# Four graph layers on one core: the first layer's opening in three pieces of nodes, its degree sums started by copies, its biases loaded behind eight tiles

## The reference

```python
h = relu((x - mean(x)) / sqrt(var(x) + 1e-5)); x = x + relu((adj @ h) @ W0.T + b0)      # layer 0
h = relu(layernorm(x)); x = x + lorentz_attention(h, adj, W1, Wq, Wk, scales)            # layer 1
h = relu(layernorm(x)); x = x + expmap0((adj / deg aggregated logmap(h)) @ W2 + b2)      # layer 2, deg = adj.sum(1)
h = relu(layernorm(x)); x = x + rank_weights(adj != 0) @ (h @ W3) + b3                   # layer 3
```

## Time and profile before

| what | value |
|---|---|
| three runs, us | 1113.17, 1118.21, 1117.3; median 1117.3 |
| profiled execution, us | 1117.34, span 1115.6 |
| granted PE clock, mean | 0.975 |
| busy: PE, DVE, ACT, POOL, us | 1038.4, 865.2, 757.6, 272.7 |
| DMA | 240.42 MB, mean 215 GB/s |
| first layer, tiles 0 to 63 | from 15.15 to 262.8 us |

### The profile page before, as it was taken

One profiled execution on the slowest core, in us unless ns is written; L12 is line 12 of the kernel. 1 busy time (PEld: TensorE's weight loads), 2 busy tenths in 40 slices (PEclk: granted clock), 3 DMA queues, 4 the chain that ended last, 5 costly groups with the idle time before them and its releaser, 6 DMA issues.

```text
span 1115.6 us, 14859 instructions
## 1 busy us (share of the span) xinstructions
PE 1038.4 (93%) x5404; PEld 457.0 (41%) x5404; DVE 865.2 (78%) x1011; ACT 757.6 (68%) x803; POOL 272.7 (24%) x145
## 2 busy tenths in 40 slices
PE   4899999999669999999998998999999998989998
PEld 1233333336643333333333443444544454436544
DVE  6999989996476666688668977877779887778781
ACT  2454554543355666686688889888888888777782
POOL 3179300000010000004005364444343433330010
PEclk9999999998879999999999999999999999989999
DMA  7999999991008888787764444555545545446451
GB/s 264 409 390 351 355 355 317 356 363 56 1 4 298 279 287 283 260 277 272 256 198 140 145 132 158 181 176 170 183 151 189 161 160 189 132 145 223 133 180 39
DMA packets 98438, 240.42 MB, mean 215 GB/s; under 512 B 16449, under 2 KB 47169, under 8 KB 81985
## 3 DMA queue, kind: packets, MB, share of 16 engines
q1 hardware_dynamic: 89152, 222.72, 58.1%
q10 hardware_dynamic: 9216, 16.78, 3.9%
HBM read 221.65 MB, written 17.83 MB: 215 GB/s over the span
## 4 chain that ended last, share of the span: by engine, by line
PE 49%; issue 22%; POOL 13%; DVE 9%; ACT 5%; DMA 1%; SPq 1%; POOLq 0%; DVEq 0%; ACTq 0%
PE PS L555 35%; POOL ring L533 10%; PE PS L701 5%; PE PS L702 5%; POOL H L533 2%; DVE TB L1445 1%; DMA ring<-in_adj_t 1%; ACT work L1105 1%; PE PS L567 1%; DVE work L1894 1%; PE PS L589 1%; PE PS L579 1%; DVE work L1440 1%; PE PS L831 1%; ACT work L1008 1%
## 5 line engine op out<-in xcount | busy, mean ns | idle before, releaser
L1571 DVE TENSOR_TENSOR work<-work,ring 128x1024 f32<-128x1024 f32 x128 | 151.1, 1223 | 78.7 <-ACT work L1105 78.7
L1042 ACT ACTIVATE work<-PS 128x1024 uint8<-128x1024 f32 x128 | 124.1, 1020 | 120.3 <-PE PS L555 120.3
L1105 ACT ACTIVATE work<-PS,att_sc 128x1024 f32<-128x1024 f32 x128 | 147.5, 1201 | 80.3 <-PE PS L702 72.7
L555 PE MATMUL PS<-ring,work 128*65 128x256 f32 (+1 forms) x612 | 194.1, 466 | 2.2 <-DVE work L1922 1.2
L533 POOL TENSOR_TENSOR ring<-work,ring 128x1024 f32<-128x1024 f32 (+1 forms) x57 | 134.0, 2352 | 245.7 <-DVE work L1894 245.6
L555 PE MATMUL PS<-work 128*64 128x512 f32 (+3 forms) x800 | 153.6, 524 | 1.1 <-ACT work L1168 1.0
L1888 DVE SCALAR_TENSOR_TENSOR work<-PS,work 128x1024 f32<-128x1024 f32 x72 | 85.8, 1192 | 56.4 <-PE PS L555 49.9
L555 PEld LDWEIGHTS PS<-ring,work 128*65 128x65 f32 x612 | 83.5, 140 | 91.8 <-issue 66.9
L701 PE MATMUL PS<-work 128*128 128x512 f16 x256 | 98.8, 386 | 4.2 <-DVE work L1394 2.5
L1174 ACT ACTIVATE work<-work 128x1024 f32<-128x1024 f32 x72 | 74.2, 1031 | 37.2 <-DVE work L1882 37.2
L702 PE MATMUL PS<-work 128*128 128x512 f16 x256 | 98.2, 383 | 0.0
(11 more groups left out here) (248 smaller groups left out, 1488.9 us busy)
## 6 DMA issues: line engine op xcount, KB each, us to landing
ring<-in_adj_t SPq DMA_DIRECT2D x96, 1024.0 KB, 5.2
ring<-in_adj_t SPq DMA_DIRECT2D x107, 512.0 KB, 3.8
work<-in_adj_t SPq DMA_DIRECT2D x32, 1024.0 KB, 7.6
codes<-work ACTq DMA_DIRECT2D x64, 256.0 KB, 6.6
ring<-codes SPq DMA_DIRECT2D x64, 256.0 KB, 3.8
H<-in_adj_t SPq DMA_DIRECT2D x25, 512.0 KB, 3.8
X<-in_x SPq DMA_DIRECT2D x2, 512.0 KB, 5.2
out_x<-X SPq DMA_DIRECT2D x1, 512.0 KB, 3.8
```

The source lines that it names most:

```text
L555: return mm(out_ap, lhsT, rhs, start=starts, stop=True, skip_group_check=True)
L1042: nc.scalar.activation(made[:, k, u * UNIT:(u + 1) * UNIT], PS[:, (4 + 2 * u) * BANK:(6 + 2 * u) * BANK], ACT.Relu).then_inc(sem("codes_ma ...
L1105: nc.scalar.activation(att[:, u, :], PS[:, (4 + 2 * u) * BANK:(6 + 2 * u) * BANK], ACT.Sigmoid, bias=att_sc[:, 2:3], scale=att_sc[:, 1:2]) ...
L1571: V.tensor_tensor(prob[:, m % 4, :], att[:, u, :], ring[:, s % RING, u * UNIT:(u + 1) * UNIT], ALU.mult)\
```

## The change

X is loaded and normalised in three pieces, tiles of nodes 24 to 31, 16 to 23 and 0 to 15, and the loads of pieces and adj tiles alternate. PE waits for the pieces at steps 0, 8 and 16. The biases and scalars are loaded behind the eighth tile. The clearing of TB is gone: ACT copies tile 0 into TB and DVE copies tile 32, instead of adding them; all other sums stand two tiles behind their masks, in the loop too. PE runs ten products into an unused PSUM bank before the first tile (`keep_at_work`). The wait of ACT for the scalars moves from behind code 3 to behind code 6. The rest renumbers the semaphore counts of the normalisation.

```diff
+PIECES = ((24, 32), (16, 24), (0, 16))
-            for g in (1, 0):
-                sp.dma_start(grp(X, g), grp(x_nodes, g)).then_inc(sem(f"x_loaded{g}"), 16)
             for k in range(RING0):
+                if k < len(PIECES):
+                    sp.dma_start(piece(X, k), piece(x_nodes, k)).then_inc(sem(f"x_loaded{k}"), 16)
                 sp.dma_start(ring0(k), tile0(0, T - 1 - k)).then_inc(sem(f"adj_loaded{k}"), 16)
-                if k == 1:
-                    for n, bsrc in enumerate((b0, b1, bq, bk, b2, b3)):
-                        sp.dma_start(bias[:, n, :], bsrc.partition_broadcast(P)).then_inc(sem("biases_loaded"), 16)
-                    sp.dma_start(scal[:, :], scalars.partition_broadcast(P)).then_inc(sem("biases_loaded"), 16)
+            for n, bsrc in enumerate((b0, b1, bq, bk, b2, b3)):
+                sp.dma_start(bias[:, n, :], bsrc.partition_broadcast(P)).then_inc(sem("biases_loaded"), 16)
+            sp.dma_start(scal[:, :], scalars.partition_broadcast(P)).then_inc(sem("biases_loaded"), 16)
...
-            nc.gpsimd.memset(TB[:, :], 0.0).then_inc(sem("consts_ready"), 1)
...
+            def keep_at_work(bank):
+                mm(banks(bank, bank + 1), tri_rest[:, :], tri_above[:, :].unsqueeze(1).broadcast_to([P, BANK // P, P]),
+                   start=True, stop=True)
             pe.wait_ge(sem("consts_ready"), 6)
+            for _ in range(10):
+                keep_at_work(7)
...
-                if first and h == 0 or s == TG:
-                    pe.wait_ge(sem("feats0_ready"), 1 + s // TG)
+                if s in (0, TG // 2, TG):
+                    pe.wait_ge(sem("feats0_ready"), 1 + s // (TG // 2))
...
+            square_first(0)
+            root_first(0)
+            square_first(1)
+            one("deg_added", TB[:, 0:HALF], ring0(0), ACT.Copy, ("adj_loaded0", 16))
+            root_first(1)
...
-                    if not h and k == 0:
-                        one("ln_sq", grp(sqr, 0), grp(cen, 0), ACT.Square, ("ln_centred", 2))
-                    if not h and k == 1:
-                        power_of("ln_sd", st[2], st[1], -0.5, "ln_var", 1, (0,))
-                    if not h and k == 3:
+                    if not h and k == 2:
+                        square_first(2)
+                    if not h and k == 5:
+                        root_first(2)
+                    if not h and k == 6:
                         one("scales_ready", esc[:, :], scal[:, 0:3], ACT.Exp, ("biases_loaded", 16 * 7))
...
             mask0(0, 0, 16, True)
             mask0(1, 1, 16, True)
-            centre_first(0)
+            spread_first(1)
             mask0(2, 2, 16, True)
-            degree0(0, 0, 0)
-            spread_first(0)
+            feats_first(1)
             mask0(3, 3, 16, True)
             degree0(0, 1, 1)
-            feats_first(0)
+            sums_first(2)
+            centre_first(2)
             for k in range(4, RING0):
                 mask0(k, k, 16, False)
                 degree0(0, k - 2, k - 2)
-            for k in range(RING0 - 2, RING0):
-                degree0(0, k, k)
+                if k == 5:
+                    spread_first(2)
+            feats_first(2)
...
-                        tile0(h, it * RING0 + (h * T + k), k, it * 16 + (h * T // RING0 + 1) * 16, False)
+                        mask0(it * RING0 + (h * T + k), k, it * 16 + (h * T // RING0 + 1) * 16, False)
+                        degree0(h, it * RING0 + (h * T + k - 2), (k - 2) % RING0)
+            for k in (RING0 - 2, RING0 - 1):
+                degree0(1, 2 * T - RING0 + k, k)
```

More of the change, by code:

```diff
@@ L293, in part, with piece, over_piece @@
             return ap[:, a:b]
+        def piece(ap, n):
+            a, b = PIECES[n]
+            return ap[:, a:b]
+        def over_piece(v, n):
+            a, b = PIECES[n]
+            return piece(v, n).unsqueeze(2).broadcast_to([P, b - a, D])
         def over_part(v, q):
@@ L1023, in norm @@
                 for g in groups:
-                    one("ln_sq", grp(sqr, g), grp(cen, g), ACT.Square, ("ln_centred", L * G + g + 1))
-                power_of("ln_sd", st[2], st[1], -0.5, "ln_var", L * G, groups)
+                    one("ln_sq", grp(sqr, g), grp(cen, g), ACT.Square, ("ln_centred", L * G + 1 + g + 1))
+                power_of("ln_sd", st[2], st[1], -0.5, "ln_var", L * G + 1, groups)
             nc.scalar.preload_act_table_set("natural_log_exp_and_others")
@@ L1032, in flipped_out, with square_first, root_first @@
                 one("flip_out", TA[:, g * UNIT:(g + 1) * UNIT], PS[:, g * UNIT:(g + 1) * UNIT], ACT.Copy, ("flipped", n * G + g + 1))
-            one("ln_sq", grp(sqr, 1), grp(cen, 1), ACT.Square, ("ln_centred", 1))
-            power_of("ln_sd", st[2], st[1], -0.5, "ln_var", 0, (1,))
+            def square_first(n):
+                one("ln_sq", piece(sqr, n), piece(cen, n), ACT.Square, ("ln_centred", n + 1))
+            def root_first(n):
+                act.wait_ge(sem("ln_var"), n + 1)
+                nc.scalar.activation(piece(st[2], n), piece(st[1], n), ACT.Ln).then_inc(sem("act_chain"), 1)
+                chain[0] += 1
+                act.wait_ge(sem("act_chain"), chain[0])
+                nc.scalar.activation(piece(st[2], n), piece(st[2], n), ACT.Exp, scale=-0.5).then_inc(sem("ln_sd"), 1)
+            square_first(0)
[3 more added lines that the diff above has]
+            root_first(1)
             def make_code(h, s, k, at, stored):
@@ L1122, in first_half1 @@
                 if o == 11:
-                    one("ln_sq", grp(sqr, 0), grp(cen, 0), ACT.Square, ("ln_centred", 2 * G + 1))
+                    one("ln_sq", grp(sqr, 0), grp(cen, 0), ACT.Square, ("ln_centred", 2 * G + 1 + 1))
                 if o == 12:
-                    root_of("ln_sd", "ln_var", 2 * G, 0)
+                    root_of("ln_sd", "ln_var", 2 * G + 1, 0)
                 if o == 14:
@@ L1152, in second_half2 @@
                 if n == 8:
-                    one("ln_sq", grp(sqr, 1), grp(cen, 1), ACT.Square, ("ln_centred", 2 * G + 2))
+                    one("ln_sq", grp(sqr, 1), grp(cen, 1), ACT.Square, ("ln_centred", 2 * G + 1 + 2))
                 if n == 9:
-                    power_of("ln_sd", st[2], st[1], -0.5, "ln_var", 2 * G + 1, (1,))
+                    power_of("ln_sd", st[2], st[1], -0.5, "ln_var", 2 * G + 1 + 1, (1,))
                 if n == 10:
@@ L1210, in ln_square @@
             def ln_square(q):
-                one("ln_sq", part(sqr, q), part(cen, q), ACT.Square, ("ln_centred", 3 * G + q + 1))
+                one("ln_sq", part(sqr, q), part(cen, q), ACT.Square, ("ln_centred", 3 * G + 1 + q + 1))
             def part_a(q, k):
@@ L1329, in link @@
                 dve.wait_ge(sem("dve_chain"), chain[0])
-            last = [0] * G
+            last = [0] * len(PIECES)
             def hold(g):
@@ L1394, in copy_out @@
                 V.tensor_copy(dst, src).then_inc(sem(name), 1)
[L1397 to L1418, removed]
+            def sums_first(n):
+                dve.wait_ge(sem(f"x_loaded{n}"), 16)
+                chained(n, V.reduce_sum(piece(st[0], n), piece(X, n), AX.X))
+                hold(n)
+                chained(n, V.tensor_scalar(piece(st[0], n), piece(st[0], n), -1.0 / D, None, ALU.mult))
@@ new lines, in centre_first, with spread_first, feats_first @@
+            def centre_first(n):
+                hold(n)
+                V.tensor_tensor(piece(cen, n), piece(X, n), over_piece(st[0], n), ALU.add).then_inc(sem("ln_centred"), 1)
+            def spread_first(n):
+                dve.wait_ge(sem("ln_sq"), n + 1)
+                chained(n, V.reduce_sum(piece(st[1], n), piece(sqr, n), AX.X))
+                hold(n)
+                V.tensor_scalar(piece(st[1], n), piece(st[1], n), 1.0 / D, EPS, ALU.mult, ALU.add).then_inc(sem("ln_var"), 1)
+            def feats_first(n):
+                x, root = piece(st[9], n), piece(st[2], n)
+                dve.wait_ge(sem("ln_sd"), n + 1)
+                chained(n, V.tensor_tensor(x, root, root, ALU.mult))
+                hold(n)
+                chained(n, V.tensor_tensor(x, x, piece(st[1], n), ALU.mult))
+                hold(n)
+                chained(n, V.tensor_scalar(x, x, -0.5, 1.5, ALU.mult, ALU.add))
+                hold(n)
+                chained(n, V.tensor_tensor(root, root, x, ALU.mult))
+                hold(n)
+                V.scalar_tensor_tensor(piece(H, n)[:, :, 0:D], piece(cen, n), 0.0, over_piece(st[2], n), ALU.max, ALU.mult)\
+                 .then_inc(sem("feats0_ready"), 1)
@@ L1420, in _ @@
+            sums_first(0)
+            centre_first(0)
             sums_first(1)
-            means_first(1)
+            spread_first(0)
             centre_first(1)
[L1423 to L1426, removed]
+            feats_first(0)
             def update0(g):
```

35 lines of the change are left out of this document (18 added, 17 removed).

## The result

The changed kernel takes 1107.28 us (median of 4 runs, 1105.4 to 1108.98) against 1116.24 before. The ratio is 0.9921, 95% interval 0.9896 to 0.9946: 9.0 us less, where 12.4 were forecast (1105). The profiled execution took 1108.45 us, span 1106.7, 8.9 less than before. The opening ends with the start of tile 10: 52.07 us instead of 60.30, so 8.2 of the 8.9 us are won there, and from tile 10 to the end both kernels take the same within 0.7 us (1055.3 before, 1054.6 now; span less start of tile 10).

The account below looks back on a forecast made before the run. PE's tile stream bounds from 53.68 to 264 us, load then DVE work before; opening gains 3.45 + 2.25 + 1.0 + 5.7 = 12.4 take 1117.3 to 1104.9, say 1105; range 1102 to 1108 (0.64), wider range 1100 to 1112.

Parts of the forecast that it names:

- Start of tile 0: PE's first tile starts at 11.7 us, 3.45 earlier, needing less X; bounds 10.7 to 13.5.
- tile 2: PE starts tile 2 at 18.0 us, 6.3 after tile 0 instead of 8.55: 2.25 gained.
- tile 7's successor: PE starts tile 8 at 40.2 us, tiles 2 to 7 taking 3.70 each: 1.0 gained.
- masks 7 and 8 on DVE: Mask 7 done at 36.4 us, mask 8 at 41.7, 0.8 before PE asks; tiles 8 and 9 gain 5.7.
- PE's level in tile 0: PE assumed at its 2.4 GHz level in tile 0; the slow level would lose 1.74 us.
- step 5: Tile 8's load lands at about 38.8 us, 1.2 later for two more code stores, 1.8 before DVE asks.
- rival A: Bias loads make tile 8 land late, PE stalls about 3 us: gain some 8, 1109; chance with B 0.22.
- POOL's burst: Four bias pieces due at once near mask 8 cost DVE 1.1 us, PE 0.3; by the skill's rule about 4.
- From tile 10 on: PE does the same matmuls; buffers come free 6.7 us later, taken as costing nothing.
- Rival C: Buffers freed later let loads and code stores pace 54 tiles: 21 us lost, 1126; chance 0.05.
- B: PE slow at tile 0, piece 1 late, ACT passes it on: 3.5 to 4.5 lost, 1109; with rival A 0.22.
- D: Something unseen, such as a late piece 2, costs as much as is won: 1116 to 1118; chance 0.09.

Follow-up runs that it names:

- e2: The changed kernel with only the twelve weight loads moved behind tile 15; one run, profiled span 1105.1 us.
- e3: The changed kernel with only the bias and scalar loads moved behind tile 15 and ACT's exponential of the scalars into the second half; one run, profiled span 1105.4 us.
- e5: e3 with 14 products instead of 10 ahead of tile 0; 1104.88 us, ratio to before 0.9881.
- e6: e5 with DVE finishing piece 0 first, the third piece's features behind mask 10, eight products, X load and ACT reordered; 1103.88 us, ratio to before 0.9873.
- e4: The changed kernel with the bias and scalar loads back behind the second tile; 1114.06 us, ratio to before 0.9969.
- e8: The changed kernel with the six bias loads reading 128 different rows of x, biases unused; 1103.38 us, not compared as the result differs.
- e11: The changed kernel profiled once more with nothing changed; one run, profiled span 1105.7 us.
- e1: The changed kernel with biases, scalars and weights loaded behind tile 15 and ACT's exponential of the scalars in the second half; 1108.33 us, ratio to before 0.9921.
- e9: e5 with the degree sums directly behind their own masks again; one run, profiled span 1108.5 us.

## Why the prediction was right, and where it was not

- **Start of tile 0** (forecast 11.7, measured 11.81), **tile 2** (18.0, 18.35), **tile 7's successor** (40.2, would have been 40.55), **masks 7 and 8 on DVE** (mask 7 starting at 35.3, measured 35.26; mask 8 at 40.6, or 41.7 with POOL's 1.1, and it would have been 41.7): right to within 0.4 us. The working by bytes and rates placed piece 1 at 7.8, DVE moved at 8.05. Tile 2 is right in part by luck: code 0 came when forecast (15.22), but PE did not wait 0.6 for it; tile 1 simply took the usual 3.70, where the forecast has 3.1 and the wait.
- **PE's level in tile 0** was assumed fast and was so in the changed kernel (1.94 us), but it was a close thing. In these executions PE was fast after rests of 1.03 to 2.11 us and slow after 2.18 and more; a rest of 2.09 and one of 2.18 came out on different sides. From tile 0 to tile 2 the slow level costs 1.6 to 2.6 us (8.1 to 9.2 instead of 6.54), and it stays lost where nothing else is waited for. The forecast took the ten products to put PE at its fast level; the last section says what the rows show of that.
- **Load of tile 8**, step 5: wrong, and 3.8 of the 4.2 us between the forecast gain (12.4) and the timeline's (8.2) are there: 2.48 of wait and 1.64 of slow PE, less the stall of 0.3 that had been reckoned. I had tile 8 land at 29.82 + 7.8 = 37.6 before and 1.2 us later after. The 7.8 was the median of all loads of L375 to 120 us. The load of tile 8 itself took, in the trace of before:

```profile
DMA to landing us min/median/max: 11.7/11.7/11.7
```

So it landed at 41.5, which nobody noticed as mask 8 was held until 52.41 by the sums. 41.5 + 1.2 = 42.7, and it was 42.9: the change of 1.2 was right as a number, the starting point was not. Whether the two code stores made the 1.2 is not shown, as the load was also issued 3.46 us later and took 9.6 instead of 11.7. With it the forecast would have been a wait of 2.4 us at tile 8 and a slow PE behind it (1.6), a gain of 8.7 and 1108.6: rival A, whose condition (a landing from 41.4 on) was met without a longer hole, and whose "gain is some 8" came. So the time is near the forecast because this one step cost 3.8 us and not more; the account of tile 8 was rival A's.
- **POOL's burst** (0.3 us of stall): it came at 36.56 and stretched DVE's steps (the third piece's features 1.41 instead of 1.22, mask 9 1.94 us), but the load hid it: not a term of the result. (The piece beside mask 9 is POOL's fifth, at 45.59.) In e2, with the load in time, mask 8 came 1.1 us later than in e3, where POOL was quiet (41.85 against 40.73), just the 1.1 of the forecast. Two of e2's rows, one of POOL and one of DVE:

```profile
38.60 0.62 POOL L486 CAST bcut<-bias 128x384 bf16<-128x384 f32 x1
38.77 0.47 DVE L1449 TENSOR_TENSOR st<-st 128x16 f32<-128x16 f32 x1
```

By the Trainium skill (SBUF — State Buffer, "Who interferes with whom") whichever of the two issues first keeps the shared ports for its whole instruction and blocks the other. The trace agrees: DVE's step, 0.17 us long in e3, ends with POOL's cast (39.24 and 39.22), and the step at 39.49 with POOL's next (40.27 and 40.23). Yet DVE loses only what is left of a piece when its own instruction comes up. So the four pieces, 2.5 us long in e2, cost it 1.1 and not their whole length, which the prediction had taken from that rule for its stall of 4.
- **From tile 10 on**: nothing lost, as said. Rival C (the ring) is refuted by e5 and e6: their tiles follow at 3.70 us, with the same lag of the sums. Rivals B and D did not happen.
- **End of the layer**: sums 61 to 63 end 1.2 us before PE's last features end, so they delay nothing, as reckoned (DVE waited 5.85 there before, 1.20 after).
- **The bounds**: a start at 13.5 (1.8 us less), the slow level (1.74) and a stall of 4 instead of 0.3 (3.7) take the 12.4 down to 5.2, not to the 7 that the prediction gives. The measured 9.0 lies in both ranges.

## What to carry to other kernels

Take the duration of a load from its own issue, at the place that matters: the first loads behind a burst of small ones took 11.7 and 13.1 us where the median was 7.8, and a landing that nothing waits for shows in no view of waits. A stall removed at one place is won only as far as the next late thing allows, so list what lands just behind it; here a late mask hid a late load, and moving the slow bias loads from one side of the opening to the other moved their hole right ahead of the load that was needed next. Keep loads that read one small row into 128 partitions off any path that is waited for: behind tile 7 their hole still met tile 8 (42.9), behind tile 15 it met nothing. And read a thing that hangs on a tenth of a microsecond in more than one trace: PE's level in tile 0 came out fast in some and slow in others.

## What the runs showed of the hardware that I had not expected

- Seven loads that each spread one small row over 128 partitions, 0.2 MB in all, held the core's transfers low for some 6 us: 67 GB/s at a share of 0.22 before (12 to 18 us), 69 at 0.27 in the changed kernel (30 to 36), 75 at 0.26 in e4 (9 to 15), 119 at 0.34 in e3 (54 to 60). While six loads of 256-byte pieces from different rows passed, they moved 274 to 333 GB/s (e8).
- Ten products and a rest of 2.09 us (e11) or 2.11 (e4) were followed by a fast tile 0, ten products and a rest of 2.18 (e1) by a slow one. In these three, and in the changed kernel, all ten products themselves ran at the slow level (one every 0.43 us, 4.45 in all), so they did not leave PE fast: the rise came after them or not at all. In e2, e3 and e8 the last of the ten already ran fast (3.82, 4.07 and 4.20 us in all), and tile 0 was slow after rests of 2.27 to 2.85. What decides there stays open. The clock rows show the 1.2 GHz level as 0.50 in e2 and e3 (13 to 15 us) but 1.00 in e1, where the same matmuls took 3.68 us; so the levels here go by the durations.
- A short POOL instruction can take very long beside a DVE that never rests. In the kernel before, one copy of a single row took 53.86 us (from 62.40), in e3 a cast took 31.05 (from 63.53) and in e9 one took 58.57, where the same cast took 0.62 in e2. Before and in e3, DVE's masks and sums followed each other every 3.34 us throughout, and POOL's instruction ended just after a mask that started 0.1 us later than the others do (115.91 and 94.23). Why it came in at once in the changed kernel (1.18, 0.78 and 2.57 us), where DVE was busy for 59.5 of 60 us too, isn't shown. Nobody waited for these pieces in any kernel here.
